# A chain of four graph networks: bias products from one table of levels, and layer 2's narrow product turned in the node pass

## The chip, the cores and the metric

One Trainium2 chip, one core. The metric is the device time of one execution in microseconds. Six engines matter: PE (TensorE; its weight loads are listed as PEld), ACT (ScalarE), DVE (VectorE), POOL (GpSimd), and SP (SyncE), which issues transfers.

## The reference

50,000 nodes with 128 features, 25,000 edges (`src`, `dst`, sorted by `dst`) with 64 edge features. Four layers, each followed by a residual and a norm over the 128 features:

```python
x = _layernorm(x + _L0_gnn_ref(...))   # attention with edge features, then h = [out, x] @ W1 + b1, norm * ln_g + ln_b, relu, @ W2 + b2
x = _layernorm(x + _L1_gnn_ref(...))   # 4 heads, every node is its own neighbour too; + bias, norm * gamma + beta, gelu
x = _layernorm(x + _L2_gnn_ref(...))   # two attention layers, 8 heads x 16, elu, then 1 head x 64 (Wl2, bl2, bias2), elu, elu(h @ Wlin + blin)
x = _layernorm(x + _L3_gnn_ref(...))   # 4 heads with edge features, no self loops
```

More than half of the nodes have no incoming edge. For such a node each layer needs only the node itself: in layer 0 `out` is zero, in layers 1 and 2 the attention over itself alone gives weight 1. In layer 2, z = x @ Wl1 + bl1 + bias1, h = elu(z), xl = h @ Wl2 + bl2, h3 = elu(xl + bias2).

## The kernel before

**Stages.** `prepare` loads weights and indices and makes derived weights. `node_pass` computes all four layers for all nodes as if they had no edges, and writes the tables x1, x2, xl2, x3 and the output. `slot_pass` runs five times (layers 0, 1, 2a, 2b, 3) over the 25,000 edges, sorted by target, and overwrites rows of nodes that do have edges. Between stages all engines meet at a barrier.

**prepare.** SP issues 62 transfers (the list `loads`, line 430), all counted on one semaphore. DVE, PE and POOL start their work on them when all have landed; POOL's constants come from memset, iota and affine_select and need none. DVE derives the weights. The five row biases (`b1_rows`, `b2_rows`, `bias_rows`, `bl2_rows`, `xlr_rows`) are made there: a bias is loaded to all 128 partitions, centred, split three times into a bf16 part and a remainder (lines 554 to 565), and the parts are written to partitions 0, 32 and 64 of a 128 x 512 bf16 tile.

**Bias products.** `pe_rows` (lines 211 to 222) makes four row tiles of 128 nodes in one PSUM bank. With a bias it first issues one bf16 product of `ones` (stationary, 128 x 128) and the bias tile (128 x 512), then adds four (or eight) fp32 products.

**node_pass.** A chunk is 512 nodes. Seven streams u = 0 to 6 each have a PSUM bank and buffers, and one turn of the loop works on seven chunks; 14 turns, 98 chunks. `NODE_CHAIN` lists the steps of one chunk with their engines. The order of the steps on each engine is written out by `order_of_work`: a sort of the start times in `PLAN["node"]`, shifted by one period for each stream; a step whose time falls behind the turn runs one turn later. Each engine takes its steps strictly in that order, with semaphore waits on the steps that it depends on. The unit of the times has no influence, only their order has.

Steps that matter here: `sq0` to `sq3` are four squares on ACT each, which sum a row's squares; the row scale is then made either on ACT by Ln and Exp (`norm_on_act`: sq0, sq2) or on POOL by an addition and a power of −0.5 (`norm_on_pool`: sq1, sq3). `z0`, `x1`, `z1`, `x2` on DVE scale the rows; `z0T`, `x1T`, `z1T`, `x2T` on PE turn them. `gelu1` needs a table of its own on ACT, so there is a table load ahead of it and one behind it. The narrow product of layer 2 was made with nodes in the partitions, and then turned:

```python
elif step == "xl":       # PE: bias product and 4 products of 64 columns
    pe.wait_ge(*g.DVE.done(u, i, "h2"))
    pe_rows(pe, g, u, A, [(act_T[u], c.Wl2[:, :])], c.bl2_rows, C2)
elif step == "z3":       # PE: 4 turns of 128 x 64, after ACT copied xl to SBUF
    pe.wait_ge(*g.ACT.done(u, i, "xl"))
```

`exp3` (ACT), `h3_em1` and `h3` (DVE) make the elu of it, `z4` (PE) multiplies by Wlin, then `exp4`, `h4`, `y2T`, `y2` follow. `store_xl` on SP writes the rows of xl. POOL also has side work in each chunk: two indirect gathers (line 1014) and two indirect scatters (line 1018).

Of the kernel before, what the change touches and what calls it, by code (L numbers as in the profile page):

```python
# [76 lines left out]
class Steps:  # L77
# [12 lines left out]
    def before(self, u, i):  # L90
# [6 lines left out]
        "node": (41.623, (9.764, 46.736, 34.596, 46.244, 59.089, 52.055, 90.616, 79.284, 106.659, 110.082, 95.014, 96.156,  # L97
# [94 lines left out]

def tiles_of(t):
    return t.rearrange("p (t n) -> p t n", t=TILES)
# [91 lines left out]
def prepare(nc, a, c, dram, ctx):  # L286
# [3 lines left out]
    loads = []  # L290

    def load(name, shape, src, dt=F32, room=None):
        t = (room or sb)(name, shape, dt)
        loads.append((t[:], src))
        return t

    def column(name, src, m=P):
        return load(name, [m, 1], src.rearrange("(p o) -> p o", o=1))

    def row(name, src, m=P):  # L300
        return load(name, [P, m], src.partition_broadcast(P))
# [6 lines left out]

# [4 lines left out]
    loads.append((c.We0[0:EF, :], a["L0_gnn_We0"]))  # L313
    loads.append((c.We1[0:EF, :], a["L0_gnn_We1"]))
    c.W = load("W", [P, D], a["L1_gnn_W"])
    c.Wl1 = load("Wl1", [P, D], a["L2_gnn_Wl1"])
    c.Wr1 = load("Wr1", [P, D], a["L2_gnn_Wr1"])
    c.Wl2 = load("Wl2", [P, C2], a["L2_gnn_Wl2"])
    c.Wr2 = load("Wr2", [P, C2], a["L2_gnn_Wr2"])
    c.Wlin = load("Wlin", [C2, D], a["L2_gnn_Wlin"])  # L320
    c.WnT = load("WnT", [P, D], a["W_node_T"])

    c.ln_g = column("ln_g", a["L0_gnn_ln_g"])
    c.ln_b = column("ln_b", a["L0_gnn_ln_b"])
    c.gamma = column("gamma", a["L1_gnn_gamma"])
    c.beta = column("beta", a["L1_gnn_beta"])
    c.bl1 = column("bl1", a["L2_gnn_bl1"])
    br1 = column("br1", a["L2_gnn_br1"])
    c.bias1 = column("bias1", a["L2_gnn_bias1"])
    c.bl2 = column("bl2", a["L2_gnn_bl2"], C2)  # L330
    c.br2 = column("br2", a["L2_gnn_br2"], C2)
    c.bias2 = column("bias2", a["L2_gnn_bias2"], C2)
    c.blin = column("blin", a["L2_gnn_blin"])


# [3 lines left out]
    c.ones = sb("ones", [P, CHUNK], BF16)  # L339
    c.minus_half = sb("minus_half", [P, TILES])  # L340
    c.eps = sb("eps", [P, TILES])
    c.minus_one = sb("minus_one", [P, CHUNK])
# [15 lines left out]
    c.b1_rows, c.b2_rows, c.bias_rows = (sb(n, [P, CHUNK], BF16) for n in ("b1_rows", "b2_rows", "bias_rows"))  # L358
    c.bl2_rows = sb("bl2_rows", [P, TILES * C2], BF16)
    c.xlr_rows = sb("xlr_rows", [P, CHUNK], BF16)  # L360
    c.src_cols = load("src_cols", [P, SLOT_TILES], a["src_cols"], I32)
    c.src_back_cols = sb("src_back_cols", [P, SLOT_TILES], I32)
    c.dst_gather_cols = load("dst_gather_cols", [P, SLOT_TILES], a["dst_gather_cols"], I32)
# [5 lines left out]

# [47 lines left out]
    with own:  # L417
# [9 lines left out]
        def _(sp):  # L427
            with nc.allow_non_contiguous_dma("a few vectors"):
                for dst, src in loads:
                    sp.dma_start(dst, src).then_inc(loaded, 16)  # L430
# [1451 lines left out]
```

## Time and profile before

| | |
|---|---|
| median of 3 runs | 3930.91 us (3929.29 to 3931.96) |
| the profiled execution | 3930.92 us, span 3929.2 us |
| busy over the span | PE 88%, DVE 88%, ACT 76%, PEld 62%, POOL 58% |
| preparation | 0 to 68 us |
| node pass | 68 to 1,229 us |
| slot passes | 1,229 us to the end |

The span runs from the first to the last instruction. Busy time of PE is modelled at its ends, so an engine shown at 99% has no time left for more work. The start times of neighbouring instructions are the better measure of what one costs, since they overlap on all engines.

### The profile page before, as it was taken

How to read it: one execution, taken by the hardware profiler on the slowest of the kernel's cores; microseconds unless marked ns; L12 is line 12 of the kernel's file. 1: busy time of each engine (PE TensorE's matmuls, PEld its weight loads, DVE VectorE, ACT ScalarE, POOL GpSimd, SP SyncE). 2: the span in 40 equal slices, each digit the busy share in tenths (PEclk: the TensorE clock that was granted, in tenths of full speed). 3: DMA queues.
4: the chain of work that ended last, by engine and by line, in shares of the span. 5: the costliest groups of instructions: out<-in, count | busy, mean ns of one | idle time of the engine just before them, and what ended most of it. 6: DMA issues, size and time to landing. Idle time of an engine off the chain costs nothing. (4 is left out here: it accounts for less than half of the span.)

```text
span 3929.2 us, 70937 instructions
## 1 busy us (share of the span) xinstructions
PE 3463.5 (88%) x19239; PEld 2424.3 (62%) x19434; DVE 3443.5 (88%) x6459; ACT 2988.0 (76%) x10008; POOL 2266.1 (58%) x2305
## 2 busy tenths in 40 slices
PE   2999999999995999996999978999969999678775
PEld 2888888888883666664666644545535555355443
DVE  3899999999995999996999977999969999699886
ACT  1999999999994999984898875666648888454443
POOL 1577777777776777624555505444334443477777
PEclk9999999999997999998999998999979999899998
DMA  1455555555554444423554425555535555455442
GB/s 47 124 156 146 152 156 149 149 156 148 149 151 116 113 113 113 106 80 107 129 127 124 126 55 143 139 145 139 127 100 155 157 158 156 110 141 143 123 121 72
DMA packets 719118, 503.42 MB, mean 128 GB/s; under 512 B 141745, under 2 KB 621335, under 8 KB 718960
## 3 DMA queue, kind: packets, MB, share of 16 engines
q1 hardware_dynamic: 533072, 362.39, 33.7%
q0 software_dynamic: 56528, 81.64, 8.5%
q10 hardware_dynamic: 129360, 57.82, 5.3%
q14 instruction: 124, 1.02, 0.1%
q8 instruction: 34, 0.56, 0.1%
HBM read 304.28 MB, written 200.10 MB: 128 GB/s over the span
## 5 line engine op out<-in xcount | busy, mean ns | idle before, releaser
L237 ACT ACTIVATE node_z<-psum 128x128 f32<-128x128 f32 x1568 | 419.0, 325 | 22.2 <-PE psum L217 13.1
L1204 POOL DMA_INDIRECT slot2a_src_rows<-x,src_table_cols x196 | 236.3, 1205 | 307.3 <-PE psum L226 178.6
L659 ACT ACT_TABLE_LOAD x305 | 391.3, 1283 | 5.4
L237 ACT ACTIVATION_READ_ACCUMULATOR node_z<-psum 128x1 f32 x1568 | 348.2, 227 | 0.0
L1204 POOL DMA_INDIRECT slot_src_rows<-x,map_cols x196 | 202.2, 1032 | 251.7 <-PE psum L226 124.6
L1204 POOL DMA_INDIRECT slot2b_src_rows<-xl,map_cols x196 | 190.5, 972 | 232.8 <-PE psum L226 186.5
L237 ACT ACTIVATE slot_logit<-psum 128x128 f32<-128x128 f32 x980 | 256.5, 278 | 85.7 <-PE psum L217 55.6
L1208 POOL DMA_INDIRECT slot_dst_rows<-in_x,dst_gather_cols x196 | 213.5, 1090 | 120.6 <-PE psum L226 59.7
L1204 POOL DMA_INDIRECT slot_src_rows<-x,src_table_cols x196 | 203.4, 1038 | 127.4 <-POOLq L250 68.0
L1014 POOL DMA_INDIRECT node_gathered<-in_x,src_cols x196 | 236.2, 1205 | 47.1 <-issue 47.1
L1238 POOL DMA_INDIRECT out_nodes<-slot_new,out_index x196 | 217.9, 1112 | 60.1 <-issue 60.1
L1018 POOL DMA_INDIRECT slot_map<-payload,out_index x196 | 202.7, 1034 | 59.7 <-issue 59.7
L1199 POOL DMA_INDIRECT map_cols<-slot_map,src_back_cols x196 | 202.5, 1033 | 59.7 <-issue 59.7
L231 ACT ACTIVATE slot_expo<-slot_expo 128x1024 f32<-128x1024 f32 x196 | 184.9, 943 | 65.4 <-DVE slot_expo L1664 64.6
L909 DVE TENSOR_TENSOR node_x<-psum,node_rstd 128x512 f32<-128x512 f32 x294 | 201.2, 684 | 32.3 <-POOL node_rstd L1005 27.6
L217 PE MATMUL psum<-center,node_act_T 128*128 128x128 f32 x1568 | 210.2, 277 | 3.2 <-DVE node_act_T L974 2.2
L1005 POOL TENSOR_TENSOR node_rstd<-node_variance,minus_half 128x4 f32<-128x4 f32 x196 | 200.7, 1024 | 15.4
L237 ACT ACTIVATION_READ_ACCUMULATOR slot_logit<-psum 128x1 f32 x980 | 205.5, 210 | 0.0
L1671 DVE TENSOR_TENSOR_SCAN slot_den<-slot_expo,slot_den 128x512 f32<-128x512 f32 x147 | 187.1, 1273 | 11.5 <-ACT slot_expo L231 9.2
L217 PEld LDWEIGHTS psum<-center,node_act_T 128*128 128x128 f32 x1568 | 192.1, 193 | 6.5 <-DVE node_act_T L974 4.0
L1687 DVE TENSOR_TENSOR_SCAN slot_num<-slot_expo,slot_num,slot_t 128x512 f32<-128x512 f32 x147 | 187.5, 1276 | 1.4
L1002 POOL TENSOR_TENSOR node_variance<-node_mean_square,eps 128x4 f32<-128x4 f32 x196 | 49.5, 253 | 241.2 <-ACT node_z L237 241.2
(422 smaller groups left out, 12070.4 us busy)
## 6 DMA issues: line engine op xcount, KB each, us to landing
x<-node_x SPq DMA_DIRECT2D x294, 256.0 KB, 3.0
slot_neg<-neg SPq DMA_DIRECT2D x147, 256.0 KB, 4.9
node_xT<-in_x_T SPq DMA_DIRECT2D x98, 256.0 KB, 3.1
out_nodes<-node_x SPq DMA_DIRECT2D x98, 256.0 KB, 2.8
x<-slot_new ACTq DMA_DIRECT2D x98, 256.0 KB, 2.4
slot_keep<-keep SPq DMA_DIRECT2D x98, 256.0 KB, 4.2
slot_dst_rows<-x SPq DMA_DIRECT2D x98, 256.0 KB, 5.4
xl<-node_xl SPq DMA_DIRECT2D x98, 128.0 KB, 2.7
```

Of the source, the lines that this page charges most:

```text
L217: ins = pe.matmul(bank(u)[:, tile_cols(t, width)], tile[:, tile_cols(t)], weights, start=bias is None and k == 0, stop=k == len(parts) - 1 ...
L237: ins = act.activation(g.z[u][:, t, :], rows[:, t, :], ACT.Square, scale=float(D ** -0.5), accum_out=sums[u][:, t:t + 1])
L659: act.add_instruction(mybir.InstLoadActFuncSet(name=nc.get_next_instruction_name(), ins=[], outs=[], act_func_set_id=wanted[0]))
L909: v.tensor_tensor(out[:, :, :], source, rstd[:, :].unsqueeze(2).broadcast_to([P, TILES, D]), ALU.mult)\
L1005: pool.tensor_tensor(g.rstd[u][:, :], g.variance[u][:, :], c.minus_half[:, :], ALU.pow).then_inc(g.pool_out[u], 1)
L1014: pool.indirect_dma_start(gathered[u][:, t, :], None, a["x"], at_index(c.src_cols[:, tile:tile + 1], 0))\
L1018: pool.indirect_dma_start(dram.slot_map, at_index(c.out_index[:, tile:tile + 1], 0), c.payload[:, tile, :], None, bounds_check=N - 1, oob_ ...
L1199: pool.indirect_dma_start(c.map_cols[:, tile, :], None, dram.slot_map, at_index(c.src_back_cols[:, tile:tile + 1], 0)).then_inc(signal, 16)
L1204: pool.indirect_dma_start(src_rows[u][:, t, 0:src_width], None, table, at_index(rows[:, tile, 0:1], 0))\
L1208: pool.indirect_dma_start(dst_rows[u][:, t, :], None, a["x"], column(c.dst_gather_cols, u, i, t))\
L1238: pool.indirect_dma_start(a["out"], column(c.out_index, u, i, t), new[u][:, t, :], None, bounds_check=N - 1, oob_is_err=False).then_inc(st ...
L1687: ins = v.tensor_tensor_scan(num[u][:, :], expo[u][:, 1, :], t1[u][:, :], before, ALU.mult, ALU.add)
```

## The change

- **prepare.** The transfers are in three groups (`rows`, `first`, `late`) with a semaphore each. SP issues the rows and every second one of the others (33), ACT's queue the rest (27). Instructions wait for the group that they need, and DVE's, PE's and POOL's instructions are put in another order. The five biases are columns, centred by a product with `center`, split into bf16 parts as columns of one small tile `bias_parts`, turned by one product, and copied into one 128 x 512 tile `bias_levels` (15 rows used). `level_of` holds for each bias a 128 x 128 stationary tile with ones in its three rows.
- **pe_rows.** The bias product takes `level_of` of that bias and `bias_levels`; it still contracts 128 rows.
- **node_pass, layer 2.** `z3` makes the product turned at once: Wl2 stationary, 512 nodes moving, 64 partitions out, no bias product. `exp3` and `h3` take bl2 + bias2. A new step `xlT` on ACT copies it with bl2 added to `xlT` in SBUF (64 x 512). `xl` on PE turns it back into rows after `h4`, then ACT copies and SP stores it. `y2` waits for that copy, `h3` for `xlT`.
- **node_pass, layer 1.** The root of `sq2` goes from ACT to POOL.
- **PLAN["node"]** has new times for 65 steps; its period is given as 10 (it was 41.623).
- The slot passes change only in the operands of their bias products.

```diff
-        "node": (41.623, (9.764, 46.736, 34.596, 46.244, 59.089, 52.055, 90.616, 79.284, 106.659, 110.082, 95.014, 96.156,
...
+        "node": (10.000, (0.000, 9.751, 11.069, 13.695, 14.225, 7.603, 19.906, 17.248, 22.879, 22.044, 26.547, 28.087, 19.229, 59.184,
+              30.990, 22.329, 32.796, 30.756, 36.445, 36.445, 25.495, 38.039, 35.810, 29.270, 41.486, 37.853, 45.216,
+              45.216, 34.630, 46.693, 45.863, 35.624, 49.535, 46.796, 43.350, 43.834, 55.672, 53.766, 53.766, 48.539,
+              50.068, 62.699, 59.233, 54.040, 64.580, 63.229, 68.849, 55.074, 66.341, 63.150, 63.518, 69.281, 70.984,
+              64.125, 76.204, 64.125, 64.911, 77.947, 67.096, 78.455, 2.407, 43.229, 71.576, 71.950, 61.352)),
...
-        pe.matmul(bank(u)[:, 0:TILES * width], g.c.ones[:, 0:P], bias[:, 0:TILES * width], start=True, stop=False)
+        levels = tiles_of(g.c.bias_levels[:, :])[:, :, 0:width]
+        pe.matmul(bank(u)[:, 0:TILES * width].rearrange("p (t n) -> p t n", t=TILES), g.c.level_of[:, ROW_BIASES.index(bias), :], levels,
+                  start=True, stop=False)
...
+    c.bias_levels, c.level_of = sb("bias_levels", [P, CHUNK], BF16), sb("level_of", [P, len(ROW_BIASES), P], BF16)
...
+    by_sp = loads["rows"] + loads["first"][0::2] + loads["late"][0::2]
+    by_act = loads["first"][1::2] + loads["late"][1::2]
...
+                for item in by_sp:
+                    sp.dma_start(*item).then_inc(arrived[group_of[id(item)]], 16)
...
+                for item in by_act:
+                    act.dma_start(*item).then_inc(arrived[group_of[id(item)]], 16)
...
+            v.wait_ge(sums_ready, 1)
+            did(v.tensor_copy(biases[:, 0:3], psum[:, 6, D:D + 3]))
+            did(v.tensor_copy(biases[:, 3:4], wide_bl2[:, :]))
+            biases_at = did(v.tensor_tensor(biases[:, 4:5], wide_bl2[:, :], psum[:, 6, 0:1], ALU.subtract))
...
+            n = did(v.tensor_copy(bias_parts[:, :, 0], biases[:, :]))
...
+            v.wait_ge(arrived["late"], everything["late"])
+            did(v.tensor_tensor(c.Wlr1[:, :], c.Wl1[:, :], c.Wr1[:, :], ALU.add))
+            v.wait_ge(worked, n)
+            marks["parts"] = did(v.tensor_copy(bias_parts[:, :, 2], bias_rest[1][:, :]))
+            v.wait_ge(made, marks["made"])
+            n = did(v.tensor_scalar(c.S1[:, :], same_head[8][:, :], vectors["att1"][:, 0:1], None, ALU.mult))
...
+            v.wait_ge(levels_ready, 1)
+            did(v.tensor_copy(tiles_of(c.bias_levels[0:LEVELS, :]), psum[0:LEVELS, 6, 2 * D:3 * D].unsqueeze(1).broadcast_to([LEVELS, TILES, D])))
...
+            pe.matmul(psum[0:LEVELS, 6, 2 * D:3 * D], bias_parts[:, :, :].rearrange("p k l -> p (k l)"), ident_half[:, :],
+                      start=True, stop=True).then_inc(levels_ready, 1)
...
-    norm_on_pool("sq1", "x1") + [("SP", "store_x1"), ("PE", "x1T"), ("DVE", "x1T"), ("PE", "h1")] + norm_on_act("sq2", "z1") + \
+    norm_on_pool("sq1", "x1") + [("SP", "store_x1"), ("PE", "x1T"), ("DVE", "x1T"), ("PE", "h1")] + norm_on_pool("sq2", "z1") + \
     [("PE", "z1T"), ("ACT", "gelu1"), ("DVE", "y1T"), ("PE", "y1")] + norm_on_pool("sq3", "x2") + \
     [("SP", "store_x2"), ("PE", "x2T"), ("DVE", "x2T"), ("PE", "z2"), ("ACT", "exp2"), ("DVE", "h2_em1"), ("DVE", "h2"),
-     ("PE", "xl"), ("ACT", "xl"), ("SP", "store_xl"), ("PE", "z3"), ("ACT", "exp3"), ("DVE", "h3_em1"), ("DVE", "h3"),
-     ("PE", "z4"), ("ACT", "exp4"), ("DVE", "h4"), ("DVE", "y2T"), ("PE", "y2")] + \
+     ("PE", "z3"), ("ACT", "exp3"), ("ACT", "xlT"), ("DVE", "h3_em1"), ("DVE", "h3"),
+     ("PE", "z4"), ("ACT", "exp4"), ("DVE", "h4"), ("PE", "xl"), ("ACT", "xl"), ("SP", "store_xl"), ("DVE", "y2T"), ("PE", "y2")] + \
...
-                    act_copy(act, g, u, expz[u][0:C2, :], A(u)[0:C2, :], ACT.Exp, c.bias2[:, 0:1])
+                    act_copy(act, g, u, expz[u][0:C2, :], A(u)[0:C2, :], ACT.Exp, c.node_bias2[:, 0:1])
+                elif step == "xlT":
+                    act.wait_ge(*g.PE.done(u, i, "z3"))
+                    act_copy(act, g, u, xlT[u][:, :], A(u)[0:C2, :], ACT.Identity, c.bl2[:, 0:1])
...
+                elif step == "z3":
+                    pe.wait_ge(*g.DVE.done(u, i, "h2"))
+                    pe.matmul(A(u)[0:C2, :], c.Wl2[:, :], act_T[u][:, :], start=True, stop=True).then_inc(g.pe_out[u], 1)
                 elif step == "xl":
-                    pe.wait_ge(*g.DVE.done(u, i, "h2"))
-                    pe_rows(pe, g, u, A, [(act_T[u], c.Wl2[:, :])], c.bl2_rows, C2)
-                elif step == "z3":
-                    pe.wait_ge(*g.ACT.done(u, i, "xl"))
-                    pe.matmul(A(u)[0:C2, tile_cols(0)], xl[u][:, 0, :], c.ident[:, :], start=True, stop=True)
+                    pe.wait_ge(*g.DVE.done(u, i, "h4"))
+                    pe.matmul(A(u)[:, tile_cols(0, C2)], xlT[u][:, tile_cols(0)], c.ident[0:C2, 0:C2], start=True, stop=True)
                     for t in range(1, TILES):
-                        ins = pe.transpose(A(u)[0:C2, tile_cols(t)], xl[u][:, t, :], c.ident[:, :])
+                        ins = pe.transpose(A(u)[:, tile_cols(t, C2)], xlT[u][:, tile_cols(t)], c.ident[0:C2, 0:C2])
                     ins.then_inc(g.pe_out[u], 1)
                 elif step == "z4":
...
-                    v.wait_ge(*g.ACT.done(u, i, "sq2_rstd"))
+                    v.wait_ge(*g.POOL.done(u, i, "sq2_rstd"))
...
-                    elu(u, i, C2, "h3_em1", c.bias2, h3)
+                    v.wait_ge(*g.ACT.done(u, i, "xlT"))
+                    elu(u, i, C2, "h3_em1", c.node_bias2, h3)
```

## Rows read from the trace of the kernel before

**Rows 1.** Stretches: start:end, length, busy time by engine (instructions), PE clock, DMA share, GB/s
```profile
0.00:36.00 36.00, 0.00 (x0) 0.00 (x0) 0.57 (x1) 0.00 (x0) 11.29 (x40) 1.00 0.31 73
36.00:68.00 32.00, 7.78 (x28) 5.18 (x28) 25.86 (x130) 0.00 (x0) 0.00 (x0) 1.00 0.04 13
...
229.00:1100.00 871.00, 862.13 (x6469) 747.13 (x6546) 798.96 (x2003) 848.99 (x3543) 619.95 (x693) 1.00 0.53 151
```

**Rows 2.** Timeline of the preparation: start, duration, engine, line, tiles
```profile
0.82 0.39 SPq L430 DMA_DIRECT2D Wq<-in_L_gnn_Wq  x1
...
31.42 0.65 SPq L430 DMA_DIRECT2D row_prev<-in_dst_prev_rows  x2
35.43 1.28 DVE L478 TENSOR_TENSOR keep_r<-row_here,row_prev 49x512 f32<-49x512 int32 x2 [35.43 <-DMA row_prev<-in_dst_prev_rows]
```

**Rows 3.** The same, later in the preparation and at the node pass's first instruction
```profile
48.38 0.73 DVE L554 CAST part<-row_f 128x128 bf16<-128x128 f32 x5
...
55.56 0.28 DVE L559 COPY xlr_rows<-part 1x512 bf16<-1x512 bf16 x1
...
59.47 0.29 DVE L578 COPY Wsa<-psum 128x128 f32<-128x128 f32 x1 [2.79 <-PE psum L632]
...
68.03 1.28 ACT L237 ACT_TABLE_LOAD   x1 [68.03 <-PEq L417]
```

**Rows 4.** Issues of node_xT, seven chunks apart (one turn of the loop)
```profile
199.96 0.40 SPq L758 DMA_DIRECT2D node_xT<-in_x_T  x1
...
279.12 0.40 SPq L758 DMA_DIRECT2D node_xT<-in_x_T  x1
```

**Rows 5.** Timeline of PE in one chunk of the node pass
```profile
637.69 1.02 PE L887 MATMUL psum<-node_h,Wlin_full 65*128 65x512 f32 x2
638.55 0.27 PE L214 MATMUL psum<-bl_rows,ones 128*128 128x256 bf16 x1
...
639.50 0.38 PE L214 MATMUL psum<-b_rows,ones 128*128 128x512 bf16 x1
...
641.59 0.43 PE L880 MATMUL psum<-ident,node_xl 128*64 128x128 f32 x2
641.96 0.52 PE L882 MATMUL psum<-ident,node_xl 128*64 128x128 f32 x3
642.31 0.60 PE L226 MATMUL psum<-ident,node_x 128*128 128x128 f32 x4
```

**Rows 6.** Timeline of ACT in the same chunk
```profile
638.04 0.31 ACT L237 ACTIVATE node_z<-psum 128x128 f32<-128x128 f32 x1
...
639.04 0.76 ACT L231 ACTIVATE node_z<-psum,minus_one_col 128x512 f32<-128x512 f32 x1
639.61 0.35 ACT L237 ACTIVATE node_z<-psum 128x128 f32<-128x128 f32 x1
...
640.55 0.54 ACT L231 ACTIVATE node_variance<-psum,eps 128x4 f32<-128x4 f32 x2
640.99 0.38 ACT L231 ACTIVATE node_xl<-psum 128x256 f32<-128x256 f32 x1
641.25 0.30 ACT L231 ACTIVATE node_rstd<-node_variance 128x4 f32<-128x4 f32 x2
...
646.80 0.69 ACT L231 ACTIVATE node_z<-psum,node_bias 128x512 f32<-128x512 f32 x1
647.38 0.29 ACT L231 ACTIVATE node_variance<-node_moments,eps 128x4 f32<-128x4 f32 x1
```

**Rows 7.** Groups of POOL, 300 to 1,100 us: count, busy us, mean ns, idle
```profile
L1014 POOL DMA_INDIRECT node_gathered<-in_x,src_cols x142 | 172.1, 1212 | 34.0 <-issue 34.0
...
L1018 POOL DMA_INDIRECT slot_map<-payload,out_index x140 | 144.4, 1032 | 42.7 <-issue 42.7
L1008 POOL TENSOR_TENSOR node_rstd<-node_var,minus_half 128x4 f32<-128x4 f32 x71 | 71.5, 1006 | 0.0
L1002 POOL TENSOR_TENSOR node_variance<-node_mean_square,eps 128x4 f32<-128x4 f32 x142 | 36.5, 257 | 143.0 <-ACT node_z L237 143.0
```

More of the change, by code:

```diff
@@ L190 @@
 UNCOUNTED = ("store", "gather", "put", "dst_gather", "scatter")
+ROW_BIASES = ("b1", "b2", "bias", "bl2", "xlr")
+LEVELS = 3 * len(ROW_BIASES)
 def tiles_of(t):
@@ L288, in sb, with fetch, load, column @@
         return ctx.enter_context(nc.sbuf_tensor(name, shape, dt))
-    loads = []
-    def load(name, shape, src, dt=F32, room=None):
+    loads = {"rows": [], "first": [], "late": []}
+    def fetch(into, src, group):
+        loads[group].append((into, src))
+    def load(name, shape, src, dt=F32, room=None, group="late"):
         t = (room or sb)(name, shape, dt)
-        loads.append((t[:], src))
+        fetch(t[:], src, group)
         return t
[L297 to L301, printed above, removed]
+    def column(name, src, m=P, group="late"):
+        return load(name, [m, 1], src.rearrange("(p o) -> p o", o=1), group=group)
     own = ExitStack()
@@ L312, in prepare @@
     c.We0, c.We1 = sb("We0", [P, D]), sb("We1", [P, D])
[L313 to L333, printed above, removed]
+    fetch(c.We0[0:EF, :], a["L0_gnn_We0"], "late")
+    fetch(c.We1[0:EF, :], a["L0_gnn_We1"], "late")
+    c.dst_gather_cols = load("dst_gather_cols", [P, SLOT_TILES], a["dst_gather_cols"], I32)
     c.ident = sb("ident", [P, P])
@@ L474, in _, with did @@
         def _(v):
-            v.wait_ge(loaded, 16 * len(loads))
+            count = [0]
+            def did(ins):
+                ins.then_inc(worked, 1)
+                count[0] += 1
+                return count[0]
+            for t in (wide_bl2[C2:, :], c.We0[EF:, :], c.We1[EF:, :]):
+                did(v.memset(t, 0.0))
+            v.wait_ge(arrived["rows"], everything["rows"])
             for o in range(2):
                 v.tensor_tensor(keep[o][:, :], row_here[o][:, :], row_prev[o][:, :], ALU.is_equal).then_inc(masks, 1)
+            v.wait_ge(counted, 2)
@@ new lines, in _ @@
+            marks["src_float"] = count[0]
+            flags_at = [did(v.tensor_tensor(c.last[o][:, :], here[o][:, :], after[o][:, :], ALU.not_equal)) for o in range(2)][0]
+            v.wait_ge(levels_ready, 1)
+            did(v.tensor_copy(tiles_of(c.bias_levels[0:LEVELS, :]), psum[0:LEVELS, 6, 2 * D:3 * D].unsqueeze(1).broadcast_to([LEVELS, TILES, D])))
+            v.wait_ge(worked, n)
+            did(v.tensor_scalar(c.own_relu[:, :], c.S1[:, :], SLOPE - 1.0, None, ALU.mult))
+            did(v.tensor_scalar(c.src_relu[:, :], c.S1[:, :], 1.0 - SLOPE, None, ALU.mult))
@@ L614, in _ @@
+            did(v.tensor_copy(c.self_dst[:, 0:C2], c.Wda[:, 0:D:2]))
+            n = did(v.tensor_tensor(c.self_dst[:, C2:], c.Wsa[:, 0:D:2], c.Wda[:, 0:D:2], ALU.add))
+            v.wait_ge(worked, n)
+            v.wait_ge(firsts, 9)
+            v.wait_ge(masks, 4)
         @block.tensor
         def _(pe):
-            pe.wait_ge(loaded, 16 * len(loads))
-            pe.wait_ge(made, 32)
-            pe.wait_ge(worked, 28)
-            pe.matmul(psum[:, 6, 0:D], all_ones[:, :], c.Wl2r2[:, :], start=True, stop=True)
@@ L633, in _ @@
-            ins.then_inc(products, 1)
+            pe.wait_ge(made, marks["ident"])
             pe.wait_ge(firsts, 2)
```

354 lines of the change are left out of this document (180 added, 174 removed), and 6 rows, old and new, of the table PLAN.

## The prediction, made before the change was run

> **What bounds the kernel now.** I read the stretches first [rows 1]. The execution has a preparation of 68 us, a node pass up to 1,229 us, and five slot passes that take the remaining 2,700 us. The diff changes instructions in the first two stages; of the slot passes it touches only the operands of the bias products. So I priced each of the first two stages by what its time is made of.
>
> In the preparation nothing computes for 36 us, and for the next 32 us only DVE is nearly full (25.9 of 32 us) [rows 1]. The timeline tells why [rows 2]. SP issues 62 transfers one after another, from 0.82 us to 31.42 + 0.65 = 32.07 us, that is 0.504 us each, and DVE's first instruction waits for the last of them, which lands at 35.43 us, 3.36 us after its issue. The DMA engines are no limit there: their mean share is 0.31. The node pass then starts at 68.03 us [rows 3].
>
> In the node pass the same chunk of work comes back every (279.12 − 199.96) / 7 = 11.31 us [rows 4]. Over 871 us PE is busy 99.0%, ACT 97.5%, DVE 91.7%, POOL 71.2%, at clock 1.00 [rows 1]. In us per chunk this is 11.19, 11.02, 10.37 and 8.05. Two engines are nearly full, PE a little more than ACT. To make the pass shorter both must lose work; adding work to ACT costs time almost at once.
>
> **The preparation, part by part.** I count 60 transfers after the change: 4 of masks and every second one of the other two groups go to SP (33), the other 27 to ACT's queue. At 0.504 us each, SP ends its issues at 0.82 + 33 × 0.504 = 17.5 us, and the last transfer lands 3.36 us later, at 20.8 us instead of 35.4. The share of 0.31 leaves room for twice the rate. The masks (4 issues) are there at about 6 us and the group "first" (13 issues on SP) at about 11 us.
>
> DVE's work is reordered so that much of it lies before the last arrival. Behind the wait for "late" I count 39 instructions; ahead of it about 50. DVE ran 130 instructions in its 32 us [rows 1], 0.247 us each with all waits. The 50 are 12.3 us from about 6 us, so they end near 18.5 us, under cover of the transfers. The 39 are 9.6 us, up to 30.4 us. The splitting of bias rows in three bf16 parts took 48.38 to about 55.83 us, 7.4 us [rows 3]; on a few columns instead of 128 x 128 tiles it is some eight small instructions, already in these counts. Behind the last wait there are products that DVE waits for. Before, that wait was 2.79 us [rows 3], and I add 2 us. With 0.5 us for the change of stages the node pass starts at 33 us: **−35 us**. Bounds: −38 (no wait shows) and −31 (the whole wait, and DVE instructions at 0.3 us because small copies out of PSUM are more frequent).
>
> One rule of the Trainium skill speaks against this part. "DMA: Bandwidth & Descriptors", section "Issuing engines are not separate DMA queues", says that transfers started on several engines share the same 16 DMA engines, and that it saves only the issuing time, which is usually small beside the transfer. Here the trace disagrees with the "usually": 31.3 us of issuing stand beside a DMA share of 0.31. What the rule would give is a rival below.
>
> **The node pass, PE.** Removed: the bias product and four products of 64 columns, 638.55 to 639.50 = 0.95 us, and z3 with four turns of 128 columns, 641.59 to 642.31 = 0.72 us [rows 5], 1.67 us together. Added: one product of 512 columns, like that of 637.69 to 638.55 = 0.86 us [rows 5], and four small turns of 64 rows. These were not seen in this form; not more than 0.72 us (the same count with twice the columns), and not less than 0.36 us (half of it, by the columns). As the stationary side has to be loaded 128 wide, I take 0.6. PE: 11.19 − 1.67 + 1.46 = 10.98 us per chunk (10.74 to 11.10). PE saves about 0.2 us and is no longer the fullest.
>
> **ACT.** Removed: layer 1's Ln and Exp on 128 x 4. A pair of Ln took 640.99 − 640.55 = 0.44 us, so 0.22 each, and a pair of Exp was busy 0.30, at most 0.15 each [rows 6]: 0.27 to 0.37 us, I take 0.32. Added: xlT, a pass of 64 x 512 out of PSUM. An activation of 512 elements lasts 647.38 − 646.80 = 0.58 us to the next start [rows 6]; 0.58 added. Its squares now add into mean_square in SBUF: four squares of that kind took 639.04 − 638.04 = 1.00 us, four that add into PSUM 640.55 − 639.61 = 0.94 us [rows 6], so +0.06. Table loads stay at two per chunk, since one gelu1 still stands alone between exponentials. ACT: 11.02 + 0.58 + 0.06 − 0.32 = 11.34 us (11.29 to 11.39). **ACT becomes the engine that sets the pass.** Before, the fullest engine idled 0.12 us per chunk (11.31 − 11.19). Half of that on top gives 11.40 us per chunk, and with 98 chunks 0.09 × 98 = **+9 us**.
>
> **POOL and DVE.** POOL gains layer 1's addition and its root. An addition is 0.26 us, a root 1.01 us [rows 7]: 1.27 us. With the gaps at its indirect transfers, (34.0 + 42.7) us in 70.7 chunks = 1.08 us [rows 7], POOL has 8.05 + 1.08 + 1.27 = 10.4 us of 11.4. It fits, with 1 us to spare. Its 143 us of waiting for ACT [rows 7] is the cover; if it were gone the root would come late at z1 on DVE, and then z1T on PE. DVE keeps its instructions; h3 has one more wait, for xlT, behind which everything placed after h3 on DVE is queued. SP's xl store moves behind h4, in a queue with time to spare (six stores and a load in 11.3 us).
>
> The new order is a set of other sort keys. Its cost I can't read from rows before; the idle share is what it changes. Below: ACT never waits, 11.29 us, −2 us. Above: every chunk has one more stall as long as half an indirect transfer with its gap (0.5 × 1.3 us), 0.3 us of which ACT makes good: +0.35 us, about +35 us. I take the stall of today's fullest engine, as said.
>
> **Bias products.** Still one bf16 product of the same size ahead of the others in h0, y0, h1 and xlr; 128 rows are contracted before and after. Zero; the operands are both 16-bit and contiguous, which excludes a gain or a loss beyond a few ns. The slot passes: zero.
>
> **Sum.** The profiled execution took 3930.9 us (span 3929.2 and 1.7 around it), the same as the median of 3930.9. 3930.9 − 35 + 9 = **3905 us**.
>
> **Rivals.**
> (a) The node pass gets no longer, or shorter: ACT's waits vanish, and the turned product helps PE as meant. For it: both engines had idle moments. Against: ACT can't go under 11.29 us. 11.29 × 98 is −2 us: 3894 us; with a preparation at its best, 3891.
> (b) The transfers come no sooner from two queues, as by the rule of the skill's page. Taken as a mechanism of this kernel: the last lands at 35.4 us as before, DVE's last 39 instructions and 2.5 us follow, the node pass starts at 47.5 us, −20.5 us: 3919 us. Against it is the DMA share of 0.31.
> (c) The new order stalls and eats the gain. The gain is used up at (35 − 9)/98 = 0.27 us more per chunk, so 11.67 us; within 0.2% from 11.58 on: 3923 to 3939 us. For it: two engines above 96% and POOL at 91% leave little to absorb a late step.
> (d) Slower: layer 1's root on POOL. It stands in one queue with four indirect transfers of 1.03 to 1.21 us plus 0.3 each [rows 7]. If z1 waits there for half an additional transfer beyond (c), 0.65 us per chunk on top of ACT's 11.34 us, a chunk takes 11.99 us: +67 us, 3963 us. It decides from 11.75 us per chunk (3939 us). Against it is 1 us of free time on POOL.
>
> **Chances.** My case (3896 to 3914) 0.52; (a) 0.19; (b) and its neighbours up to 3923 0.15; (c) 0.09; (d) 0.05. What a measurement of this kernel can tell from no change is about 0.2%, 7.9 us. Faster 0.86, the same 0.09, slower 0.05. From 3887 to 3925 us the cases hold 8 in 10 and more; the likeliest one's own range is 3896 to 3914.
>
> **What would show it.** The first node-pass instruction near 33 us; SP's and ACT's last issue near 17 us; issues of node_xT seven chunks apart by 7 × 11.40 = 79.8 us; in the node pass ACT at 99% and PE at 96 to 97%, POOL near 82% busy; xlT at 0.58 us; waits of DVE's z1 for POOL short. The slot passes should last as long as before, 2,700 us. The prediction is wrong if the turn grows by over 2 us, if it falls below 79 us, or if the last load lands later than 25 us.

## The result, and the profile after

The changed kernel takes 3918.2 us (median of 7 runs, 3912.59 to 3922.12) against 3930.91 (7 runs). The ratio is 0.9969, 95% interval 0.9958 to 0.998. It is faster, by 12.7 us where 26 were forecast. The profiled execution took 3916.04 us with a span of 3914.3 us.

The stretches of the changed kernel come first, in the columns of [rows 1]:

```profile
0.00:19.20 19.20, 2.71 (x11) 1.96 (x11) 11.71 (x50) 0.00 (x0) 12.57 (x37) 1.00 0.54 129
19.20:27.70 8.50, 5.27 (x20) 3.77 (x20) 7.86 (x39) 0.00 (x0) 0.00 (x0) 1.00 0.11 39
229.00:1100.00 871.00, 844.38 (x5720) 673.59 (x5793) 755.41 (x1929) 837.37 (x3353) 670.37 (x818) 0.99 0.62 146
```

The preparation, in the timeline: SP's last issue, DVE's first work behind the last transfer, DVE's last instruction, and the node pass's first one.

```profile
17.06 0.59 SPq L429 DMA_DIRECT2D raw_edge<-in_L_gnn_W_edge  x1
19.25 0.29 DVE L571 TENSOR_TENSOR Wlr<-Wl,Wr 128x128 f32<-128x128 f32 x1 [0.76 <-DMA raw_edge<-in_L_gnn_W_edge]
...
27.02 0.21 DVE L622 TENSOR_TENSOR self_dst<-Wsa,Wda 128x64 f32<-128x64 f32 x1
27.75 1.28 ACT L241 ACT_TABLE_LOAD   x1 [27.75 <-PEq L413]
```

The node pass starts at 27.75 us instead of 68.03 [rows 3], 40.3 us sooner. It then ends at 1,221.8 us instead of 1,229.1, so it has become 32.9 us longer (1,194.0 against 1,161.1 us). The slot passes take 2,692.5 us against 2,700.1. In the sixteen profiled executions with the new operands of the bias products they took 2,692 to 2,703 us, in the three with the old ones 2,700 to 2,706. So most of this difference is scatter; whether some 5 us of it belong to the new operands is not shown. The bias products themselves are not faster: in e1_prep_only (below) one of 512 columns takes 0.216 us to the next start, as in the kernel before. −40.3 + 32.9 − 7.6 gives the difference of the two spans, 14.9 us, but for rounding.

Where do the 33 us of the node pass arise? Here are two issues of node_xT that lie seventy chunks apart.

```profile
191.03 0.40 SPq L774 DMA_DIRECT2D node_xT<-in_x_T  x1
...
1011.02 0.40 SPq L774 DMA_DIRECT2D node_xT<-in_x_T  x1
```

That is 82.0 us for seven chunks, against 79.2 [rows 4] and a forecast of 79.8. But within the seven, most intervals are 11.2 to 11.4 us; two or three are 11.8 to 13.8. The loss comes once a turn. All engines' rows at that place, in order of time, show it:

```profile
250.88 0.72 ACT L235 ACTIVATE node_z<-psum,minus_one_col 128x512 f32<-128x512 f32 x1
251.44 0.34 ACT L235 ACTIVATE node_variance<-node_moments,eps 128x4 f32<-128x4 f32 x1
254.53 0.28 ACT L241 ACTIVATE node_z<-psum 128x128 f32<-128x128 f32 x1 [2.75 <-issue]
255.80 0.69 DVE L931 TENSOR_TENSOR node_x<-psum,node_rstd 128x512 f32<-128x512 f32 x1 [3.48 <-ACT node_rstd L235]
```

exp4 and sq4_log are the last steps of ACT's loop body, and sq2's first square is the first step of the next turn. Between them ACT does nothing for 2.75 us, and "issue" says that it waits for nothing that the profile shows. Then ACT's root of layer 4 comes late, with it x3 on DVE, and with it PE's turn of x3. The waits from 300 to 1,100 us (in total, times, longest) say that this is the rule:

```profile
DVE node_x L931 <- ACT node_rstd L235: 71.1, 69, 3.6
...
ACT node_z L241 <- issue: 23.0, 10, 2.8
PE psum L230 <- DVE node_x L931: 18.7, 10, 2.4
```

ten times in ten turns. In the kernel before, the same jump left this in ACT's timeline, behind four squares of sq3 (the fourth is the first line):

```profile
446.10 0.34 ACT L237 ACTIVATE node_z<-psum 128x128 f32<-128x128 f32 x1
...
447.36 0.69 ACT L231 ACTIVATE node_z<-psum,minus_one_col 128x512 f32<-128x512 f32 x1 [0.83 <-issue]
```

That is 0.5 to 0.8 us, once in seven chunks. [Rows 6] lie inside a turn and can't show it.

The operations that the diff brought, in groups of the changed kernel (columns as in [rows 7]):

```profile
L1028 POOL TENSOR_TENSOR node_rstd<-node_variance,minus_half 128x4 f32<-128x4 f32 x206 | 210.0, 1020 | 10.8
L235 ACT ACTIVATE node_xlT<-psum,bl 64x512 f32<-64x512 f32 x68 | 49.9, 734 | 0.0
...
L900 PE MATMUL psum<-ident,node_xlT 64*128 64x64 f32 x138 | 29.8, 296 | 0.0
L902 PE MATMUL psum<-ident,node_xlT 64*128 64x64 f32 x207 | 24.0, 223 | 0.0
```

The four small turns take (29.8 + 24.0) / 69 = 0.78 us busy in a chunk; from their first start to the next product's it is about 0.55 us, as they overlap. The timeline of a kernel with the same products that keeps PE busy (e1_after_act_straight, below) shows both new pieces between neighbouring starts: z3 from 499.57 to 500.58, the small turns from 510.27 to 510.82.

```profile
499.57 1.07 PE L900 MATMUL psum<-node_act_T,Wl 128*64 128x512 f32 x2
500.58 0.66 PE L230 MATMUL psum<-ident,node_x 128*128 128x128 f32 x4
...
510.27 0.43 PE L904 MATMUL psum<-ident,node_xlT 64*128 64x64 f32 x2
510.54 0.35 PE L906 MATMUL psum<-ident,node_xlT 64*128 64x64 f32 x3
510.82 1.07 PE L900 MATMUL psum<-node_act_T,Wl 128*64 128x512 f32 x2
```

### The profile page after: what moved, and what is told of

It is laid out like the page before. It is cut to its first block and busy times, and to the rows that moved or that the text cites. A ratio compares the mean times of both kernels' runs of the same rounds, so it can differ in the third digit from the quotient of the medians.

```text
span 3914.3 us, 69757 instructions
## 1 busy us (share of the span) xinstructions
PE 3487.7 (89%) x18556; PEld 2368.0 (60%) x18751; DVE 3418.6 (87%) x6418; ACT 3012.3 (77%) x9910; POOL 2366.6 (60%) x2498
## 5 line engine op out<-in xcount | busy, mean ns | idle before, releaser
L241 ACT ACTIVATION_READ_ACCUMULATOR node_z<-psum 128x1 f32 x1568 | 379.5, 257 | 0.0
L1028 POOL TENSOR_TENSOR node_rstd<-node_variance,minus_half 128x4 f32<-128x4 f32 x294 | 300.0, 1020 | 15.8
L1041 POOL DMA_INDIRECT slot_map<-payload,out_index x196 | 237.7, 1213 | 49.8 <-issue 49.8
L1037 POOL DMA_INDIRECT node_gathered<-in_x,src_cols x196 | 194.5, 992 | 59.6 <-issue 59.6
L221 PE MATMUL psum<-center,node_act_T 128*128 128x128 f32 x1568 | 224.2, 288 | 5.5 <-ACT node_xl L235 2.9
L235 ACT ACTIVATE slot_expo<-slot_recip 128x512 f32<-128x512 f32 x98 | 62.1, 633 | 160.4 <-DVE slot_recip L1747 160.1
```

The source lines that it names most:

```text
L221: ins = pe.matmul(bank(u)[:, tile_cols(t, width)], tile[:, tile_cols(t)], weights, start=bias is None and k == 0, stop=k == len(parts) - 1 ...
L235: act.activation(out, source, func, bias=bias, scale=scale).then_inc((done or g.act_out)[u], 1)
L241: ins = act.activation(g.z[u][:, t, :], rows[:, t, :], ACT.Square, scale=float(D ** -0.5), accum_out=sums[u][:, t:t + 1])
L1028: pool.tensor_tensor(g.rstd[u][:, :], g.variance[u][:, :], c.minus_half[:, :], ALU.pow).then_inc(g.pool_out[u], 1)
L1037: pool.indirect_dma_start(gathered[u][:, t, :], None, a["x"], at_index(c.src_cols[:, tile:tile + 1], 0))\
L1041: pool.indirect_dma_start(dram.slot_map, at_index(c.out_index[:, tile:tile + 1], 0), c.payload[:, tile, :], None, bounds_check=N - 1, oob_ ...
```

## The experiments

All are compared with the kernel before on the same chip. "Turn" is the time of seven chunks, from node_xT's issues over 63 chunks; other 63 chunks can give a turn that differs by 0.1 to 0.6 us, and by up to 1 us in some kernels with turns written out ahead of the loop, so small differences of turns say little there. The range behind a ratio is its 95% interval.

### First: the parts, and the jump

**e1_prep_only** has the new preparation and the old node pass. 

> The new preparation with the old node pass. In the trace of the changed kernel the node pass starts 40.3 us sooner (27.75 for 68.03 us) and lasts 33 us longer (1,194 for 1,161 us). Theory 1 (the parts add up; the preparation is worth all of its 40 us, and the node pass loses 27 to 33 of it): 3,891 us, turns of 79.2 us. Rival (a sooner start is given back later, or the new bias operands cost time in the node pass): 3,905 us or more, turns longer than 79.5 us.

Measured: 3898.24 us (ratio 0.991, 0.9893 to 0.9927), node pass from 27.56 us, turn 79.87. So the preparation's gain arrives, less some 12 us that the node pass grows by (1,172.7 us): PE now waits for node_xT in nearly every turn (7.5 us in ten turns, where no such wait of the kernel before was over 0.3 us), behind a slow issue on SP one chunk after SP's jump,

```profile
421.89 1.32 SPq L778 DMA_DIRECT2D x<-node_x  x1
```

where other issues take 0.37 to 0.42. The time, 3,898 us, lies between theory and rival. Against this kernel the node pass's changes cost 20 us.

The next three take loops away. The edit, for one engine or several:

```
-            with engine.Fori(1, NODE_ITERS) as i:
-                run(i, "all")
+            for i in range(1, NODE_ITERS):
+                run(i, "all")
```

**e1_after_act_straight**: the changed kernel, ACT's node turns written out. 

> The changed kernel with the node pass's 13 middle turns written out one after another on ACT alone, in place of the loop; same instructions, same order. Theory 1 (once per turn ACT stands still for 2.75 us at the loop's jump, since the last steps ahead of it were just waited for, and DVE's x3 and x2 and PE's x2T wait behind it): the gap goes, turns of 79.1 to 79.5 us in place of 82.0, time shorter by 13 x 2.6 = 34 us, 3,884 us. Rival (the gap comes from the order of steps or from layer 1's root on POOL, and the jump only marks the place): turns stay at 81.5 us or more, 3,910 us or more.

**e1_before_act_straight**: the same in the kernel before. 

> The kernel before with ACT's 13 middle node turns written out. Its gap at the jump is 0.99 us and PE, the fullest engine, loses 0.7 us there. Theory 1: turns of 78.6 us in place of 79.16, time shorter by 7 us, 3,924 us. Rival (PE is full anyway and written-out code costs ACT as much as the jump): no change, 3,931 us.

**e1_after_all_straight**: the changed kernel, with PE, DVE and SP too. 

> The changed kernel with the node pass written out on ACT, PE, DVE and SP. Theory 1: little more than with ACT alone, as the other engines' jumps lie where they had work queued or time to spare: turns of 79.0 us, 3,882 us. Rival (every engine's jump costs): turns under 78.5 us, 3,875 us or less; or, if code that is not repeated comes in too slowly for PE, gaps of PE in the middle of a turn and more time.

Measured: 3880.72 us (0.9867, 0.9851 to 0.9883), 3926.75 (0.9987, 0.9976 to 0.9997) and 3884.12 (0.988, 0.986 to 0.99). In the first the turn is 79.17 us, and the window of 300 to 1,100 us has both engines full:

```profile
300.00:1100.00 800.00, 796.30 (x5450) 634.27 (x5520) 720.18 (x1842) 795.72 (x3190) 645.10 (x778) 1.00 0.65 151
```

Nothing in the order of work was changed, so the order doesn't stall. ACT's jump alone cost 3918.2 − 3880.7 = 37.5 us (the turn shrinks by 2.8 us at each of twelve jumps back, 34 us); in the kernel before it cost 5 (3931.97 against 3926.75). The other engines' loops cost nothing that can be measured.

### Second: is it what stands ahead of the jump?

My theory was that in the kernel before four squares were queued behind which the jump went on. Both shifts leave the cyclic order as it is and move ACT's start times against the loop's end:

```
-            now = start + u // groups * groups * period
+            now = start + u // groups * groups * period + (0.9 if phase == "node" and engine == "ACT" else 0.0)
```

**e2_after_act_shift**: 

> The changed kernel with ScalarE's node steps placed one step later against its loop's end: the loop ends after sq3's four squares, and exp4 and sq4_log come first in the next turn; the cyclic order of its instructions is the same. Theory (the price of ScalarE's jump is what is not queued behind it: four squares of about 1.1 us are queued, the log had just been waited for): the gap at the jump falls from 2.75 to about 1 us, the turn from 82.0 to about 80.2 us, time about 3,895 us. Rival (the jump costs 2.75 us wherever it lies): turn 82.0 us, time 3,918 us.

**e2_before_act_shift** (−0.3): 

> The kernel before with ScalarE's node steps placed one step earlier against its loop's end: the loop ends after exp4, which waits for TensorE's z4, and sq3's squares come behind the jump; same cyclic order. Theory (what is queued hides the jump): the gap at the jump grows from 0.99 to 2 to 2.7 us, turn 80.5 to 81 us, time about 3,950 us. Rival (the old node pass does not feel where the jump lies): gap 1 us, turn 79.2 us, time 3,931 us.

Measured: 3913.49 us (0.9949, 0.9932 to 0.9966), turn 81.99; and 3963.26 us (1.0078, 1.006 to 1.0097), turn 81.8. The gap of 0.99 us that two expectations give for the kernel before is too high: the twelve in its trace are 0.54 to 0.84 us. The first run contradicts the theory: four squares stand ahead, and 2.47 us are idle.

```profile
414.14 0.30 ACT L241 ACTIVATE node_z<-psum 128x128 f32<-128x128 f32 x1
...
417.00 0.69 ACT L235 ACTIVATE node_z<-psum,minus_one_col 128x512 f32<-128x512 f32 x1 [2.47 <-issue]
```

The second run goes its way and beyond: one step moved across the jump makes the old kernel 30 us slower.

```profile
373.47 0.76 ACT L231 ACTIVATE node_z<-psum,minus_one_col 128x512 f32<-128x512 f32 x1
377.60 0.28 ACT L237 ACTIVATE node_z<-psum 128x128 f32<-128x128 f32 x1 [3.36 <-issue]
```

So what is queued isn't enough as a cause. The DMA packets of these four traces show an instruction packet that begins 1.6 to 3.0 us ahead of the first instruction behind each of these jumps, and ends 0.8 to 1.7 us ahead of it. In the kernel before it begins 0.5 to 0.8 us before ACT starts the last instruction ahead of the jump, in the other three 0.1 to 2.5 us after. So the jump appears to wait for code. Why the fetch begins sooner in the kernel before than in e2_after_act_shift, with the same four squares ahead, stays open.

**e2_root_on_act**: ACT written out, sq2's root back on ACT. 

> The changed kernel with ScalarE's node turns written out, and sq2's root back on ScalarE (a log and an exponential, sums in PSUM) instead of GpSimd. Theory (with the jump gone ScalarE's work, 11.3 us a chunk, is the bound, level with TensorE's): ScalarE's work grows by 0.25 to 0.32 us a chunk, the turn from 79.2 to about 81 us, time about 3,905 us against 3,881 without this edit. Rival (TensorE alone bounds the pass and the root's place is free): turn 79.2 us, time 3,881 us.

```
-NODE_CHAIN: norm_on_pool("sq2", "z1")
+NODE_CHAIN: norm_on_act("sq2", "z1")
```

The run also puts the sums in PSUM, gives the log and the exponential their own places in the order, and makes z1 wait for ACT.

Measured: 3903.19 us (0.9925, 0.9905 to 0.9944), turn 80.27. The root on POOL is worth 22 us once the jump is out of the way; rival (d) had it the other way round. The time is as expected, the turn is shorter than the 81 us. By start times of ACT the log and the exponential add 0.25 us a chunk, and squares that add into PSUM give 0.09 back. The rest, 0.16 us, is exactly what a chunk grows by (11.31 to 11.47 us).

**e2_prep_all_straight** and **e3_prep_act_straight**: the old node pass behind the new preparation, written out on four engines or on ACT alone. 

> New preparation with the old node pass (four squares, old order, xlT's evictions 128x512, two log/exp pairs more on ScalarE), and the node turns of ScalarE, TensorE, VectorE and SyncE written out, so that no engine jumps. Theory (the node changes have no gain of their own worth more than 2 us once no engine jumps, because the old pass was already at one engine's work): turn of seven chunks 78.6 us, node pass 1,155 us, time 3,876 to 3,884 us, the same as the changed kernel written out in the same way (3,884). Rival (the node changes do shorten the pass, and only the jump hid it): turn 79.9 us or more, time 3,895 us or more.

> New preparation, old node pass, only ScalarE's node turns written out: the pair to the changed kernel with the same edit (3,881 us). Theory (the node changes shorten the pass once ScalarE does not jump, by what TensorE's products of layer 2 lose): SyncE still jumps and TensorE waits once a turn for a load, turn 79.6 us, time about 3,895 us, so that the node changes are worth about 15 us. Rival (they are worth nothing, and the all-written-out pair differed by SyncE's fetches alone): turn 78.8 us, time about 3,882 us.

Measured: 3900.33 us (0.9915, 0.9896 to 0.9933) and 3883.45 us (0.9884, 0.9868 to 0.9901). Both theories failed: both times lie where the rivals put them. As tests of the node changes the two disagree, and the second is the fair one: in e2_prep_all_straight, SP's written-out code makes single issues take up to 2.08 us, PE waits up to 1.71 us for node_xT, and the turn is 79.56. In e3_prep_act_straight the turn is 78.88 us and PE is 99.9% busy. Against the changed node pass under the same edit (turn 79.17, 3880.72 us) the intervals overlap: the node pass's changes are worth nothing that can be measured, and a turn is 0.3 us longer with them. Layer 1's root on POOL and the turned product are both in this comparison, so the 22 us of the root only pay for what xlT and the rest add.

### Third: the number of jumps, and a better end

**e3_after_half_jumps** runs two turns in each round of ACT's loop. 

> The changed kernel with two turns of ScalarE's node work in each round of its loop (one turn, then six rounds of two), so that ScalarE jumps back 5 times instead of 12. Theory (each jump costs the pass its stall of about 2.8 us, because an instruction packet is fetched only when the sequencer gets to the jump and nothing of it is hidden): 7 jumps less, about 20 us, time about 3,898 us, between the changed kernel and the one written out (3,881). Rival (the stall comes back for fetching the longer code in line): time 3,910 us or more.

```
+                run(1, "all")
+                with engine.Fori(1, NODE_ITERS // 2) as i:
+                    run(i * 2, "all")
+                    run(i * 2 + 1, "all")
```

**e3_after_end_gelu** is the shift again, by 3.8. 

> The changed kernel with ScalarE's loop ending behind a table load and a gelu (2.1 us of work in its queue) instead of behind exp4 and sq4_log; the cyclic order is the same. Theory (the jump's fetch starts when the sequencer has got past the last wait of the loop, so work queued ahead of the jump hides it if the wait before it was met early): stall about 1 to 1.5 us, turn about 80.5 us, time about 3,900 us. Rival (what is queued hides nothing, as with sq3's squares): stall 2.2 us or more, turn 82 us, time 3,914 to 3,918 us.

Measured: 3903.83 us (0.9933, 0.9916 to 0.9949), with five gaps of 2.1 to 2.95 us in the window; and 3882.2 us (0.9878, 0.9861 to 0.9894), turn 79.17, with no gap at all. This last was more than the theory allowed. The queue of the instruction fetches tells why (packets, MB, share, 300 to 1,100 us), first the changed kernel:

```profile
q14 instruction: 57, 0.47, 0.2%
```

and the one that ends behind the gelu:

```profile
q14 instruction: 7, 0.06, 0.0%
```

It jumps as often, but hardly fetches. ACT's trace has 351 instructions from one jump to the next in both. A packet is 0.47 MB / 57 = 8.2 KB. Written out, ACT's code needs (32 − 7) packets in 10.1 turns; a turn is 322 instructions, so a packet holds about 130, say 128 (an estimate). The changed kernel fetched (57 − 7) / 9.8 = 5 packets a turn, more than the same code written out. The new theory: a body that touches few enough packets stays in the engine; this body of 351 instructions touches three packets or four, depending on where it lies.

The queue q14 is not PE's. With PE written out as well (e1_after_all_straight) another queue appears, which moves nothing in this window while PE loops; its packets have 0.72 MB / 44 = 16.4 KB:

```profile
q8 instruction: 44, 0.72, 0.4%
```

PE's trace has about 1,100 instructions a turn there, so one of these packets holds some 256.

### Fourth: the place alone

These write out some of ACT's turns ahead of an unchanged loop, which moves its body in memory (`peeled` is 4, 3, 1, 2):

```
+            for i in range(1, 1 + peeled):
+                run(i, "all")
-            with engine.Fori(1, NODE_ITERS) as i:
+            with engine.Fori(1 + peeled, NODE_ITERS) as i:
```

**e4_after_peel4**: 

> The changed kernel with four of ScalarE's node turns written out ahead of its loop, which stays as it is: same body, same end (exp4 and the log), 8 jumps instead of 12. By a count of ScalarE's instructions, the loop's body (some 346) starts 4 x 315 instructions later; if code is fetched in packets of 8 KB of 128 instructions each, this brings the start to about 21 to 31 instructions into a packet, so that the body touches three packets, as in the kernel whose loop ends behind gelu (no fetches seen there). Theory (a body within three packets stays in ScalarE's buffer and its jump costs nothing): next to no instruction packets between 300 and 1100 us, turn 79.2 us, time 3,879 to 3,885 us. Rival (what lies in the queue ahead of the jump decides, the place in memory nothing): stalls of 2 to 2.8 us as in the changed kernel, turn 82 us, 8 x 3.1 us over 3,881, about 3,906 us.

**e4_after_peel3**: 

> The same with three turns written out: 9 jumps, and the loop's body starts about 90 to 100 instructions into a packet and touches four. Both theories expect the stalls to stay: turn 82 us, 9 x 3.1 us over 3,881, about 3,909 us. A time near 3,881 would speak against the count of packets.

**e4_end_gelu_peel1**: 

> The kernel whose ScalarE loop ends behind the gelu (3,882 us), with one turn written out ahead of it: same body and end, the body's start moves from about 28 to 38 to about 87 to 97 instructions into a packet, so that it touches four. Theory (place in memory): the instruction packets come back (some 50 between 300 and 1100 us) and a stall with them; what is left of it behind 2.1 us of queued work is 0 to 1.5 us a turn, time 3,885 to 3,900 us. Rival (the loop's end alone decides): no packets, no stall, 3,882 us.

**e4_after_peel2**: 

> The changed kernel with two of ScalarE's node turns written out ahead of its loop (10 jumps instead of 12), same body and same end (exp4 and the log). By the count of instructions the body's start moves 2 x 315 on, which is 10 short of a whole number of 128-instruction packets: it comes to lie almost as in the kernel whose loop ends behind the gelu (13 instructions earlier than in the changed one), where with four turns it lay 20 short and with three 79 short. Theory (the place of the body among the packets decides whether it is fetched anew each turn): few instruction packets, no stall although exp4 and the log stand ahead of the jump, turn 79.2 us, time 3,879 to 3,885 us. Rival (only a loop that ends behind the gelu is free of it, for a reason other than its place): packets and stalls as in the changed kernel, turn 82 us, 3,912 us.

Measured: 3907.21, 3908.87, 3895.22 and 3915.71 us (ratios 0.9945, 0.9952, 0.9913, 0.9965, each ± 0.0012 to 0.0017). The first two numbers are the runs with four and three turns. The third (e4_end_gelu_peel1) agrees with the theory: the kernel without a stall gets one when its loop is only moved. It fetches 57 packets again, and leaves this:

```profile
322.68 0.78 ACT L235 ACTIVATE node_act_T<-psum,beta,gamma 128x512 f32<-128x512 f32 x1
324.40 1.28 ACT L674 ACT_TABLE_LOAD   x1 [0.94 <-issue]
```

With a table load and a gelu ahead of the jump 0.93 to 1.26 us stay visible, where exp4 and the log leave 1.7 to 3.0: so what is queued does hide part of a fetch. The two that were to lose their stall (four turns, two turns) kept it. By themselves they speak for the rival. They had been placed by a count that left out ACT's separate waits (315 for a turn; the written-out trace has 322, seven of them waits), so they didn't test the place that was meant.

**e5_peel1_pad45** and **e5_peel1_pad62**, by a full count:

```
+            for k in range(45):
+                act.activation(pad[0][:, k:k + 1], c.eps[:, 0:1], ACT.Copy)
             whole(act, run, 1)
```

> The changed kernel with one of ScalarE's node turns written out ahead of the loop and, ahead of that, 45 copies of 128x1 values that nobody reads, while ScalarE waits for the first products anyway. Body and end of the loop are the changed kernel's. A full count of ScalarE's program, waits and register instructions with it, gives 322 for a written-out turn (not 315, which put the bodies of the four earlier kernels in other places than meant: 4 to 83 instructions behind the changed kernel's place) and 351 for the loop's body. In packets of 128 instructions this one lies 17 ahead of the changed kernel's place; the kernel without a stall lies 13 ahead of it, the one whose end is shifted by one step 2 ahead. Theory (the place decides whether the body fits in three packets): few instruction packets between 300 and 1100 us, no stall at the jump, turn 79.2 us, time 3,880 to 3,888 us. Rival (only a loop that ends behind the gelu is free of it): packets and stalls, turn 82 us, about 3,915 us or more.

> The same with 62 copies, which puts the loop's body at the changed kernel's own place among the packets, 17 instructions on. Both theories expect the stalls and the packets: turn 82 us, about 3,915 us.

Measured: 3882.97 us (0.9882, 0.9865 to 0.9898), turn 79.08, no gap on ACT; and 3920.47 us (0.9971, 0.9961 to 0.998), turn 82.36. The fetch queue with 45 copies, and with 62:

```profile
q14 instruction: 7, 0.06, 0.0%
```

```profile
q14 instruction: 57, 0.47, 0.2%
```

Seventeen useless instructions more cost 37.5 us, as much as the changed kernel lost. These two kernels have the same loop and the same steps ahead of the jump, and both came out as expected; the pair shows that the place alone decides. The body's start in ACT's program, its remainder by 128, and what it did:

```
kernel                     start   mod 128   fetched anew
e5_peel1_pad45               600      88      no
e3_after_end_gelu            220      92      no
e2_after_act_shift           231     103      yes
the changed kernel           233     105      yes
e5_peel1_pad62               617     105      yes
e4_after_peel2               877     109      yes
e4_after_peel4              1521     113      yes
e4_end_gelu_peel1            542      30      yes
e4_after_peel3              1199      47      yes
```

A body of 351 (350 in e2_after_act_shift) has some 33 places in which it touches only three packets of 128. All nine rows fit one such stretch that holds 88 and 92 and ends before 103. By 256 instructions a packet no stretch fits (88 and 220 without, 105 and 241 with fetches). The old node pass, of 362 instructions at 92, was fetched anew as well (57 packets) and merely had more of it hidden. That fits too, as the longer body ends about where those of 103 and 105 do. Where a packet's border lies among these places isn't in the trace, and nothing was run between 47 and 88. So the place is shown as the cause; that it acts by three packets or four is the reading that fits, and not shown.

## Why the prediction was half right

The forecast total, −26 us, was twice what came, −12.7, and the parts were further off than the total: the node pass grew by 33 us instead of 9. That the time still came out at 3918 us is partly luck: 5 us more from the preparation and 7.6 us less in the slot passes, for which the forecast had no term, hid half of the error. By its own sign (a turn that grows by over 2 us) the prediction is wrong: the turn grew from 79.2 to 82.0 us.

**The preparation, −35 us: the mechanism was right, the gain 5 us larger.** SP's last issue came at 17.06 us as forecast, and the last load had landed at 19.2 us (forecast 20.8). Behind the last arrival DVE had 39 instructions, as counted, but they took from 19.25 to 27.23 us, 8.0 us instead of 9.6, and the 2 us for products didn't show: DVE is 92% busy in that stretch. The start was at 27.75 us instead of 33, −40.3 us. Rival (b) fell: two queues brought the last transfer to about 19 us, at a DMA share of 0.54. The Trainium skill's page "DMA: Bandwidth & Descriptors" (section "Issuing engines are not separate DMA queues") says that issuing on several engines saves only the issuing time, usually small beside the transfer. It was the issuing time that was saved here. Beside one transfer it is small in this trace too (0.50 us of 3.36), but 62 of them in a row made 31.3 us, and rival (b) made more of the page than it says.

**ACT at 11.34 us: right.** Without the jump's stall a chunk takes 79.17 / 7 = 11.31 us with ACT 99.5% busy; xlT was 0.57 us to the next start. ACT sets the pass, as said: the 0.16 us that the root adds to it in e2_root_on_act lengthen a chunk by just that. Single terms were off: the Ln and Exp are 0.25 us there and not 0.32, the squares 0.09 and not 0.06.

**PE at 10.98 us: half of the saving.** The small turns took 0.55 us for 0.6, but z3's product took 1.01 us where 0.86 was forecast from a product of 512 columns with another stationary tile. With 1.67 us removed, as read, PE's own work falls by 0.11 us a chunk instead of 0.21 (an estimate from these start times): 11.08 us, still within the stated bounds. Its busy share can't show this, as its ends are modelled: 796.3 of 800 us in the same window. PE isn't what sets the pass then, so the saving buys no time.

**The order's cost, +9 us: the step that failed.** I said that I couldn't read it from rows before, and took "the stall of today's fullest engine", 0.06 us more in each chunk. There is no such stall spread over the chunks; with ACT's fetches gone the node pass is 1,158.5 us long, 2.6 us less than before, as in rival (a). (The old node pass takes 1,155.8 to 1,157.6 us with ACT written out in the same way, so against its equal the new one is 1 to 3 us longer.) What came instead is one stall at each of the twelve jumps back, 35.6 us in all or 3.0 us each, of which 2.4 us are idle time of ACT in the mean, and it belongs neither to the order nor to the diff's operations, but to ACT's loop body having come to lie where it does, with two steps ahead of the jump that hide little. The path that the sum left out was the jump of ACT's loop. I had looked at a chunk inside the turn and never at the one with the jump, where the kernel before already showed 0.5 to 0.8 us of idle time.

**Rivals (c) and (d): fell.** 3918 us lies near (c), but no step was late by the new order. Layer 1's root on POOL saves 22 us instead of costing any (e2_root_on_act).

**The slot passes, 0: not contradicted.** They scatter by 11 us from run to run, and a gain of some 5 us can't be excluded.

## What to carry to other kernels

When an engine is full, look at its timeline across the loop's jump, and at the instruction packets of the fetch queue: a body that is fetched anew in every turn cost up to 3 us each time here, and 17 instructions more or less ahead of the loop switched this on or off. Before a change is judged, take that lottery out by writing the full engine's turns out, or compare both kernels so. If the fetch stays, long steps ahead of the jump hide a part of it: with a table load and a gelu 0.93 to 1.26 us stayed visible, with exp4 and the log 1.7 to 3.0. Four squares hid little in e2_after_act_shift (1.8 to 3.1 us stayed) and more in the kernel before (0.5 to 0.8).

## What the runs showed of the hardware that was not expected

- ACT's loop of 351 instructions is fetched anew at each turn or not at all (57 or 7 packets of 8.2 KB between 300 and 1,100 us), depending on its place (about 128 instructions a packet, an estimate from 25 packets for 10.1 turns of 322); idle at the jump is then 1.7 to 3.1 us behind short steps in the variants of the changed kernel, or none. The Trainium skill, "Runtime: NRT & Kernel Launch", section "Instruction fetch mechanics", has the rule that a jump to code outside the engine's window must wait for its fetch; the trace agrees. Its blocks of 16 KiB, 256 instructions, do not agree with ACT's packets and the table above; PE's packets (q8, in e1_after_all_straight) do have 16.4 KB.
- From the beginning of the packet to ACT's first instruction it took 1.5 to 3.0 us. A packet took 0.31 us in many cases and up to 2.04 us in others (e2_before_act_shift).
- SP's issues can be slow, too: 1.32 us and up to 1.63 behind its jump in e1_prep_only and up to 2.08 us in written-out code, against 0.37 to 0.42. In e1_prep_only an instruction packet begins 0.2 to 0.6 us ahead of each of the 13 slow ones between 300 and 1,100 us, which speaks for a wait for code but doesn't show it. In the kernel before and in the changed one none was over 0.7 us in that time.
